# Context loaded a unit at a time, single buffers for queries, keys and output, and a new order of the first units' preparation

## The chip, the cores and the metric

The kernel is one program on one core of a Trainium2 chip. Its time is the device time of one launch in microseconds (us); lower is better. Each kernel is run several times and the median is compared.

## What is computed

```python
# x: (8, 512, 2048); ctx, the context: the same shape; mask: (8, 1, 2048), all ones
x = x + tanh(g_xattn[0]) * xattn(layernorm(x), ctx, mask, Wq, bq, Wk, bk, Wv, bv, Wo, bo)
x = x + tanh(g_ffn[0]) * ffn(layernorm(x), router_weight, router_bias, expert_bias)

def xattn(qk, v, masks, ...):      # patches of 128 columns, 8 heads of 32 rows
    q = Wq @ qk_patch + bq;  k = Wk @ qk_patch + bk;  val = Wv @ v_patch + bv
    scores = q^T k / sqrt(32), masked;  attn = softmax(scores)
    return (Wo @ gelu(attn @ val) + bo) * masks

def ffn(h, ...):                   # 4096 rows of 2048; 64 experts, the best 8 kept
    scores = softmax(h @ router_weight^T + router_bias);  w = top 8 of scores, else 0
    return h * sum(w) + w @ expert_bias
```

The weight products of the attention are done in three float32r products each (high by high, low by high, high by low), so every operand of them exists as a high part (a rounding copy) and a low part (operand minus high part).

## The kernel before

A batch is one of the 8 slices of x, held whole in SBUF as `X[b % 2]`, 128 partitions by 4 tiles by 2048 columns. It is cut into 8 units of 256 columns (two patches), 64 units in all. The order of the work on each engine is fixed by a table of due times (`SLOTS`, in slots; a unit starts every 16 slots, a batch every 128; a tick is an eighth of a slot). Each engine walks the same list of ticks and issues what is due, so the table sets only the order on an engine; semaphores set the times. Unit u's due time is 16 u plus the slot of the table; in the steady state one slot is close to one microsecond.

The path of one unit:

- GpSimd normalises the columns (`z_full`); ScalarE makes `z_hi` (`z_high`), GpSimd `z_lo` (`z_low`).
- TensorE projects queries and keys (`project`); ScalarE evicts the queries into `q32` (`q_full`), VectorE the keys into `k32` (`k_full`); each has two buffers.
- SyncE loads the context a patch at a time (`load_ctx`, 256 KB, pieces of 512 bytes) into two patch buffers `cx`; ScalarE makes `cx_hi` (`c_high`), GpSimd `cx_lo` (`c_low`), TensorE the values (`v_mm`), ScalarE evicts them (`v_full`). A load waits until the low part of the patch that was in its buffer is made.
- TensorE makes the scores (`scores`), first the mask rows from `sel`, which a DMA brings from `rows_d`; VectorE takes the maxima (`top`), ScalarE the exponentials (`expo`), VectorE transposes them in blocks (`turn_p`, `turn_d`), and SyncE moves the blocks from `T` to `PT` by 16 DMAs of 80 KB (`move`).
- TensorE weighs the values by `PT` (`weigh`), VectorE divides into `o32` (`divide`, two buffers), ScalarE takes the gelu and the high part (`gelu`, `o_high`), GpSimd the low part (`o_low`), TensorE projects out (`project_out`), VectorE and GpSimd add to x (`weigh_out`, `add_x`). Statistics and router products follow.

After a batch's last unit come its router and its mixture: VectorE adds the mixture to x and SyncE stores x by 16 DMAs of 256 KB (`store`). Then the x of the batch after the next is loaded into the same buffer in eight halves of 512 KB (`load_x`, due at slot 48.5 of the next batch and every 4 slots); VectorE takes its statistics in 16 pieces (`input_stats`, from slot 63.25, every 2 slots) and then `input_norm` (slot 101.25), on VectorE the aggregates, on GpSimd the reciprocal root. SyncE's list also holds the `sel` rows, the mask (`load_weight`) and the second batch's x (from slot 21, every 7 slots).

At the start all weights pass through `X[1]`. Four blocks in the list of ticks prepare the rest of them: VectorE at `SPLIT` (the router weights' mean taken off, their low part, the output weights scaled), ScalarE at `SPLIT_A` (`wr2` high part) and `LATE_A` (`wo_hi`, `eb2`), VectorE at `LATE_V` (`wo_lo`, low part of `eb2`). `SPLIT` stands before the first `top`, and in it VectorE waits for ScalarE's `wr2`; `LATE_A` stands before the first `expo` and waits for VectorE's scaled output weights.

## Time and profile before

| | |
|---|---|
| median of 3 runs | 1191.13 us (1187.13 to 1192.66) |
| the profiled execution | 1187.5 us, its span 1185.7 us |
| busy: TensorE matmul | 1125.4 us, 95% of the span |
| busy: ScalarE, VectorE, GpSimd | 1029.7, 946.8, 715.3 us |
| DMA engines | q1, the queue of all data, 60.6% of the 16 engines' span; 199.39 MB |
| DMAs that SyncE issues | 1018 of 80 KB from T to PT, 128 context loads of 256 KB, 64 x loads, 128 stores |
| mean granted TensorE clock | 0.988 of full speed |

Busy time is a sum over an engine's instructions; an engine at 95% over the whole span can be idle for long in one stage and saturated in all others, so the stages have to be read one by one. The time of a run stands 1.8 us over the span.

### The profile page before, as it was taken

To read this page: it belongs to the slowest core of one execution; us is meant where nothing else is said; L and a number is where in the kernel's file an instruction comes from. 1 tells how busy PE (TensorE), PEld (TensorE's weight loads), DVE (VectorE), ACT (ScalarE), POOL (GpSimd) and SP (SyncE) were. 2 spreads that over 40 slices of the span, in tenths; PEclk is the share of its full clock that TensorE was granted. 3 is DMA by queue.
4 is the path that set the end of the run, shared out by engine and by line. 5 is a ranking of instruction groups with operands and counts; after the bars stand their busy time and mean duration, and the time that the engine had idled before them with its cause. 6 is when DMAs were issued, how large, how long until landed. Compare 5 with 4: busy or idle time off the path is not lost.

```text
span 1185.7 us, 32708 instructions
## 1 busy us (share of the span) xinstructions
PE 1125.4 (95%) x11661; PEld 1044.7 (88%) x11661; DVE 946.8 (80%) x1833; ACT 1029.7 (87%) x3200; POOL 715.3 (60%) x684
## 2 busy tenths in 40 slices
PE   2699999999999999999999999998999999999976
PEld 2699999899998999898998999988999899989965
DVE  6658877998789977889778987887778997787766
ACT  3688999999999899988999999997899989998954
POOL 2366767477655667567764676746766567755621
PEclk9899999999999999999999999999999999999989
DMA  9368454786548854587456865488454885555433
GB/s 289 76 176 220 117 131 126 242 211 155 132 122 259 228 129 127 149 261 191 125 129 212 237 162 128 123 259 224 102 132 121 258 232 130 127 164 179 116 83 143
DMA packets 160162, 199.39 MB, mean 168 GB/s; under 512 B 26496, under 2 KB 102272, under 8 KB 159872
## 3 DMA queue, kind: packets, MB, share of 16 engines
q1 hardware_dynamic: 158848, 196.80, 60.6%
q8 instruction: 93, 1.52, 0.5%
q10 hardware_dynamic: 1152, 0.50, 0.2%
q14 instruction: 69, 0.57, 0.2%
HBM read 79.67 MB, written 33.65 MB: 96 GB/s over the span
## 4 chain that ended last, share of the span: by engine, by line
PE 64%; SPq 9%; ACT 9%; DVE 6%; issue 4%; POOL 4%; DMA 3%; ACTq 0%; DVEq 0%; POOLq 0%
PE ring L308 8%; SPq L519 8%; PE ring L310 7%; PE ring L309 7%; PE ring L365 4%; PE ring L323 4%; PE ring L384 4%; PE ring L348 4%; PE ring L325 4%; PE ring L324 4%; PE ring L385 4%; PE ring L386 4%; ACT T L616 3%; PE ring L403 3%; PE PR L416 2%
## 5 line engine op out<-in xcount | busy, mean ns | idle before, releaser
L616 ACT ACTIVATE T<-ring,nmx 128x128 f32<-128x128 f32 x1024 | 359.6, 406 | 30.5 <-DVE nmx L769 30.3
L308 PE MATMUL ring<-z_hi,wqk_hi 128*128 128x256 f32 x1024 | 298.9, 292 | 23.7 <-DVE z_lo L951 21.6
L309 PE MATMUL ring<-z_hi,wqk_lo 128*128 128x256 f32 x1024 | 291.7, 285 | 0.0
L310 PE MATMUL ring<-z_lo,wqk_hi 128*128 128x256 f32 x1024 | 291.7, 285 | 0.0
L616 ACT ACTIVATION_READ_ACCUMULATOR T<-ring,nmx 128x1 f32 x1024 | 251.0, 245 | 0.0
L1041 POOL TENSOR_TENSOR z_lo<-z,z_hi 128x1024 fp32r<-128x1024 f32 x62 | 147.7, 2382 | 165.2 <-ACT z_hi L584 165.2
L308 PEld LDWEIGHTS ring<-z_hi,wqk_hi 128*128 128x128 f32 x1024 | 197.6, 193 | 36.5 <-DVE wqk_lo L927 21.6
L775 DVE STREAM_TRANSPOSE T<-T 128x512 f32<-128x512 f32 x256 | 171.5, 694 | 54.2 <-ACT T L616 53.7
L1053 POOL TENSOR_TENSOR X<-X,xt 128x512 f32<-128x512 f32 x128 | 165.9, 1296 | 60.7 <-DVE xt L802 60.5
L310 PEld LDWEIGHTS ring<-z_lo,wqk_hi 128*128 128x128 f32 x1024 | 198.2, 194 | 0.0
L309 PEld LDWEIGHTS ring<-z_hi,wqk_lo 128*128 128x128 f32 x1024 | 198.0, 193 | 0.0
L1047 POOL TENSOR_TENSOR cx_lo<-cx,cx_hi 128x512 fp32r<-128x512 f32 x128 | 165.7, 1295 | 43.1 <-ACT cx_hi L600 43.1
L769 DVE TENSOR_REDUCE nmx<-ring 128x4 f32<-128x512 f32 x256 | 158.7, 683 | 17.1 <-PE ring L348 17.1
L1058 POOL TENSOR_TENSOR ot_lo<-o,ot_hi 128x512 fp32r<-128x512 f32 x63 | 81.8, 1299 | 142.8 <-ACT ot_hi L643 142.8
L323 PE MATMUL ring<-wv_hi,cx_hi 128*128 128x256 f32 x512 | 146.4, 286 | 8.1 <-POOL cx_lo L1047 8.1
L802 DVE SCALAR_TENSOR_TENSOR xt<-ring,cst,mg 128x256 f32<-128x256 f32 x256 | 111.6, 478 | 47.3 <-PE ring L386 45.8
L384 PE MATMUL ring<-ot_hi,wo_hi 128*128 128x256 f32 x504 | 143.0, 284 | 2.7 <-POOL ot_lo L1058 2.1
L324 PE MATMUL ring<-wv_lo,cx_hi 128*128 128x256 f32 x512 | 145.4, 284 | 0.0
L325 PE MATMUL ring<-wv_hi,cx_lo 128*128 128x256 f32 x512 | 145.4, 284 | 0.0
L386 PE MATMUL ring<-ot_lo,wo_hi 128*128 128x256 f32 x504 | 142.6, 283 | 0.0
L385 PE MATMUL ring<-ot_hi,wo_lo 128*128 128x256 f32 x504 | 142.3, 282 | 0.0
L1034 POOL TENSOR_SCALAR z<-X,nm,rs 128x256 f32<-128x256 f32 x252 | 138.6, 567 | 0.8
(134 smaller groups left out, 2671.5 us busy)
## 6 DMA issues: line engine op xcount, KB each, us to landing
PT<-T SPq DMA_DIRECT2D x1018, 80.0 KB, 2.1
X<-in_x SPq DMA_DIRECT2D x64, 512.0 KB, 5.6
cx<-in_ctx SPq DMA_DIRECT2D x128, 256.0 KB, 3.9
out_y<-X SPq DMA_DIRECT2D x128, 256.0 KB, 3.2
mg<-in_mask SPq DMA_DIRECT2D x64, 128.0 KB, 3.6
sel<-rows_d SPq DMA_DIRECT2D x128, 3.0 KB
X<-in_eb SPq DMA_DIRECT2D x2, 512.0 KB, 8.6
X<-in_wqT SPq DMA_DIRECT2D x1, 512.0 KB, 5.2
```

What stands on the lines that cost most here:

```text
L308: e.matmul(o, wqk_hi[:, t, cols], z_hi[:, t, :], t == 0, False)
L309: e.matmul(o, wqk_lo[:, t, cols], z_hi[:, t, :], False, False)
L310: last = e.matmul(o, wqk_hi[:, t, cols], z_lo[:, t, :], False, t == DT - 1)
L323: e.matmul(o, cx_hi[:, k, :], wv_hi[:, k, :], k == 0, False)
L324: e.matmul(o, cx_hi[:, k, :], wv_lo[:, k, :], False, False)
L325: last = e.matmul(o, cx_lo[:, k, :], wv_hi[:, k, :], False, k == DT - 1)
L384: e.matmul(o, wo_hi[:, m, cols], o_hi[:, m, :], m == 0, False)
L385: e.matmul(o, wo_lo[:, m, cols], o_hi[:, m, :], False, False)
L386: last = e.matmul(o, wo_hi[:, m, cols], o_lo[:, m, :], False, m == 1)
L616: last = e.activation(T[u % 2][:, :, n, :], bank("S", 4 * u + g)[:, k * W:(k + 1) * W].rearrange("p (b j) -> p b j", b=4), ACT.Exp, bias=n ...
L775: e.transpose(blocks, blocks).then_inc(tp_v, 1)
L1053: e.tensor_tensor(xs, xs, xt[j][:], ALU.add).then_inc(x1_g, 1)
```

## The change

Seven edits:

1. `cx` becomes two buffers of a whole unit (256 columns). One DMA of 512 KB, in pieces of 1 KB, loads a unit; 64 loads in place of 128. The load of unit u + 2 stands where the load of the second patch stood and waits for both low parts of unit u. At the start both buffers are loaded, 1 MB where 512 KB were.
2. `q32`, `k32` and `o32` have one buffer each, so `q_full`, `k_full` and `divide` wait for the reader of the unit before.
3. `onef`, `wrs`, `swb` and `ex` are placed inside `L`, and `c_logits` waits for the batch before to be done with `ex`.
4. The part of VectorE's `SPLIT` block that prepares weights moves behind the first `top` (`SET_V`, tick 9), without the low part of `wr2`, which moves to `LATE_V`. So that block waits for ScalarE no more.
5. `LATE_V` moves from tick 50 to 140, behind the second unit's `top`; ScalarE's `SPLIT_A` from tick -39 to 60 and `LATE_A` from 24 to 90, both behind the first `expo`. The counts that others wait for follow (`v_w` 5 and 6 are exchanged).
6. `c_high` of patch 3 is written at a tick of its own (`CTX_A`, 39); it stood at 42, and nothing of ScalarE's list lies between.
7. The x halves are loaded from slot 50.75, every 5 slots, and their statistics taken from slot 65.75, every 2.25 slots; `input_norm` stays at 101.25.

```diff
@@ -52,9 +52,9 @@
-    sx=44.75, sx_gap=1.25, x2=45.25, rl=48.5, rl_gap=4,
-    x_1=21, x_gap=7, bn1=63.25, bn1_gap=2, norm1=101.25,
+    sx=44.75, sx_gap=1.25, x2=45.25, rl=50.75, rl_gap=5,
+    x_1=21, x_gap=7, bn1=65.75, bn1_gap=2.25, norm1=101.25,
@@ -95,7 +95,7 @@
-        NC, NV, NR, NO = 2, 4, 7, 2
+        NC, NV, NR, NO = 2, 4, 7, 1
@@ -110,11 +110,11 @@
-        cx = [sb(f"cx{i}", [128, DT, W]) for i in range(NC)]
+        cx = [sb(f"cx{i}", [128, DT, U]) for i in range(NC)]
-        q32 = [sb(f"q32_{i}", [128, 2, U]) for i in range(2)]
-        k32 = [sb(f"k32_{i}", [128, 2, U]) for i in range(2)]
+        q32 = sb("q32", [128, 2, U])
+        k32 = sb("k32", [128, 2, U])
@@ -144,20 +144,18 @@
-        swb = sb("swb", [128, NX])
+        onef, wrs, swb = L[:, 0:128], L[:, 128:128 + NX], L[:, 256:256 + NX]
-        ex = sb("ex", [128, DT, NX])
+        ex = L[:, 256:512].rearrange("p (t x) -> p t x", t=DT)
-        onef = sb("onef", [128, 128])
-        wrs = sb("wrs", [128, NX])
@@ -208,8 +206,8 @@
-        SPLIT, SPLIT_A = -48, -39
-        LATE_V, LATE_A, NEXT_A, NEXT_V = 50, 24, -40, -49
+        SPLIT, SPLIT_A, SET_V = -48, 60, 9
+        LATE_V, LATE_A, NEXT_A, NEXT_V, CTX_A = 140, 90, -40, -49, 39
@@ -345,7 +343,7 @@
-                            last = e.matmul(o, q32[u % 2][head, m, cols], k32[u % 2][head, m, cols], False, w == 1 and m == 1)
+                            last = e.matmul(o, q32[head, m, cols], k32[head, m, cols], False, w == 1 and m == 1)
@@ -408,7 +406,7 @@
-                    e.wait_ge(v_w, 5)
+                    e.wait_ge(v_w, 6)
@@ -457,7 +455,7 @@
-                    e.matmul(PR[:, 0:NX], onef[:], wrs[:], True, True).then_inc(pe_set, 1)
+                    e.matmul(PR[:, 0:NX], onef, wrs, True, True).then_inc(pe_set, 1)
@@ -487,11 +485,11 @@
-            def load_ctx(p):
-                b, w = divmod(p, S // W)
-                if p >= NC:
-                    e.wait_ge(cxlo_g, p - NC + 1)
-                e.dma_start(cx[p % NC][:], cv[b][:, :, w * W:(w + 1) * W]).then_inc(cx_in[p % NC], 16)
+            def load_ctx(u):
+                b, c = divmod(u, NU)
+                if u >= NC:
+                    e.wait_ge(cxlo_g, 2 * (u - NC) + 2)
+                e.dma_start(cx[u % NC][:], cv[b][:, :, c * U:(c + 1) * U]).then_inc(cx_in[u % NC], 16)
@@ -539,8 +537,8 @@
-            for p in range(NC):
-                load_ctx(p)
+            for u in range(NC):
+                load_ctx(u)
@@ -555,10 +553,9 @@
-                for w in range(2):
-                    for u in due(t, (8 + C["v_gap"]) * w + C["c_lo"]):
-                        if 2 * u + w + NC < TP:
-                            load_ctx(2 * u + w + NC)
+                for u in due(t, 8 + C["v_gap"] + C["c_lo"]):
+                    if u + NC < TU:
+                        load_ctx(u + NC)
@@ -584,20 +581,21 @@
-                if u >= 2:
-                    e.wait_ge(s_pe, u - 1)
+                if u:
+                    e.wait_ge(s_pe, u)
-                e.activation(q32[u % 2][:, 0, :], bank("q", u)[:, 0:U], ACT.Identity, bias=cst[:, BQ:BQ + 1])
-                e.activation(q32[u % 2][:, 1, :], bank("q", u)[:, U:2 * U], ACT.Identity,
+                e.activation(q32[:, 0, :], bank("q", u)[:, 0:U], ACT.Identity, bias=cst[:, BQ:BQ + 1])
+                e.activation(q32[:, 1, :], bank("q", u)[:, U:2 * U], ACT.Identity,
-                e.wait_ge(cx_in[p % NC], 16 * (p // NC + 1))
-                e.activation(cx_hi[:], cx[p % NC][:], ACT.Copy).then_inc(cxhi_a, 1)
+                u, w = divmod(p, 2)
+                e.wait_ge(cx_in[u % NC], 16 * (u // NC + 1))
+                e.activation(cx_hi[:], cx[u % NC][:, :, w * W:(w + 1) * W], ACT.Copy).then_inc(cxhi_a, 1)
@@ -652,6 +650,7 @@
+                    e.wait_ge(w2_v, b)
@@ -712,12 +711,14 @@
-                    e.wait_ge(v_w, 6)
+                    e.wait_ge(v_w, 5)
+                if t == CTX_A:
+                    c_high(3)
@@ -726,7 +727,8 @@
-                        c_high(2 * u + w)
+                        if 2 * u + w != 3:
+                            c_high(2 * u + w)
@@ -755,10 +757,10 @@
-                if u >= 2:
-                    e.wait_ge(s_pe, u - 1)
+                if u:
+                    e.wait_ge(s_pe, u)
-                e.tensor_tensor(k32[u % 2][:], bank("k", u)[:].rearrange("p (m i) -> p m i", m=2),
+                e.tensor_tensor(k32[:], bank("k", u)[:].rearrange("p (m i) -> p m i", m=2),
@@ -859,7 +861,7 @@
-                e.tensor_tensor(low(b), low(b), ex[:], ALU.mult).then_inc(wm_v, 1)
+                e.tensor_tensor(low(b), low(b), ex, ALU.mult).then_inc(wm_v, 1)
@@ -914,7 +916,7 @@
-            e.memset(onef[:], 1.0).then_inc(v_set, 1)
+            e.memset(onef, 1.0).then_inc(v_set, 1)
@@ -957,17 +959,15 @@
-            e.tensor_reduce(wrs[:], wrst.rearrange("p k n -> p n k"), AX.X, ALU.add).then_inc(v_m, 1)
+            e.tensor_reduce(wrs, wrst.rearrange("p k n -> p n k"), AX.X, ALU.add).then_inc(v_m, 1)
-                if t == SPLIT:
+                if t == SET_V:
-                    e.tensor_scalar(swb[:], PR[:, 0:NX], -1.0 / S, None, ALU.mult).then_inc(v_m, 1)
+                    e.tensor_scalar(swb, PR[:, 0:NX], -1.0 / S, None, ALU.mult).then_inc(v_m, 1)
-                    e.tensor_tensor(wrst, wrst, swb[:].unsqueeze(1).to_broadcast([128, SB, NX]), ALU.add).then_inc(v_m, 1)
+                    e.tensor_tensor(wrst, wrst, swb.unsqueeze(1).to_broadcast([128, SB, NX]), ALU.add).then_inc(v_m, 1)
-                    e.wait_ge(a_w, 4)
-                    e.tensor_tensor(wr2[:, :, NX:2 * NX], wrst, f32(wr2[:, :, 0:NX]), ALU.subtract).then_inc(v_w, 1)
@@ -975,6 +975,8 @@
+                    e.wait_ge(a_w, 4)
+                    e.tensor_tensor(wr2[:, :, NX:2 * NX], wrst, f32(wr2[:, :, 0:NX]), ALU.subtract).then_inc(v_w, 1)
@@ -1044,7 +1046,8 @@
-                e.tensor_tensor(cx_lo[:], cx[p % NC][:], f32(cx_hi[:]), ALU.subtract).then_inc(cxlo_g, 1)
+                u, w = divmod(p, 2)
+                e.tensor_tensor(cx_lo[:], cx[u % NC][:, :, w * W:(w + 1) * W], f32(cx_hi[:]), ALU.subtract).then_inc(cxlo_g, 1)
```

## Rows read from the trace of the kernel before

**Rows 1.** Windows of the start: length, busy (count) by engine, granted clock, DMA share, GB/s

```profile
16.00:20.00 4.00, 0.00 (x0) 0.00 (x0) 2.09 (x8) 1.38 (x2) 1.50 (x3) 1.00 1.08 349
20.00:40.00 20.00, 16.85 (x143) 16.43 (x144) 15.21 (x18) 8.62 (x15) 8.79 (x9) 1.00 0.71 164
40.00:60.00 20.00, 11.34 (x95) 10.70 (x94) 13.18 (x18) 15.74 (x68) 8.16 (x10) 0.78 0.29 76
```

**Rows 2.** Timeline of TensorE, the first units: start, length, what, idle before

```profile
33.28 1.06 PE L348 MATMUL ring<-k,q 32*128 32x128 f32 x32
...
50.07 0.55 PE L323 MATMUL ring<-wv_hi,cx_hi 128*128 128x256 f32 x1 [6.59 <-POOL cx_lo L1047]
...
56.97 0.36 PE L308 MATMUL ring<-z_hi,wqk_hi 128*128 128x256 f32 x1 [2.06 <-POOL z_lo L1041]
...
62.92 1.08 PE L365 MATMUL ring<-PT,v 128*32 128x128 f32 x32
```

**Rows 3.** Timeline of VectorE, the blocks around the first maxima

```profile
33.84 0.22 DVE L964 TENSOR_SCALAR swb<-PR 128x64 f32<-128x64 f32 x1
...
37.58 1.75 DVE L972 TENSOR_SCALAR X<-X,cst 128x1024 f32<-128x1024 f32 x1
39.26 2.47 DVE L769 TENSOR_REDUCE nmx<-ring 128x4 f32<-128x512 f32 x4
...
42.89 2.35 DVE L981 SCALAR_TENSOR_TENSOR eb<-X,cst,eb 64x2048 fp32r<-64x2048 f32 x1
```

**Rows 4.** Timeline of ScalarE, before and behind the first exponentials

```profile
39.37 1.06 ACT L716 ACTIVATE wo_hi<-X 128x1024 fp32r<-128x1024 f32 x1 [2.17 <-DVE X L972]
40.33 2.00 ACT L718 ACTIVATE eb<-X,cst 128x2048 fp32r<-128x2048 f32 x1
...
47.80 0.71 ACT L600 ACTIVATE cx_hi<-cx 128x512 fp32r<-128x512 f32 x1
...
53.29 1.05 ACT L584 ACTIVATE z_hi<-z 128x1024 fp32r<-128x1024 f32 x1
```

**Rows 5.** Timeline of SyncE's queue: the first mask rows, the first move

```profile
24.59 1.35 SPq L509 DMA_DIRECT2D sel<-rows_d  x4
...
50.43 10.82 SPq L519 DMA_DIRECT2D PT<-T  x16
```

**Rows 6.** TensorE's waits over the span: total, times, longest

```profile
PE ring L365 <- DMA PT<-T: 7.5, 7, 3.8
```

**Rows 7.** Timeline of TensorE, `weigh` of four successive units, 42 to 45

```profile
790.73 1.08 PE L365 MATMUL ring<-PT,v 128*32 128x128 f32 x32
...
806.64 1.08 PE L365 MATMUL ring<-PT,v 128*32 128x128 f32 x32
...
826.86 1.93 PE L365 MATMUL ring<-PT,v 128*32 128x128 f32 x32 [3.83 <-DMA PT<-T]
...
845.37 1.08 PE L365 MATMUL ring<-PT,v 128*32 128x128 f32 x32
```

**Rows 8.** SyncE's queue before the latest move of a batch

```profile
804.99 1.49 SPq L526 DMA_DIRECT2D X<-in_x  x3
...
809.50 0.43 SPq L494 DMA_DIRECT2D cx<-in_ctx  x1
810.04 11.01 SPq L519 DMA_DIRECT2D PT<-T  x16
```

**Rows 9.** Landing of the 16 DMAs of that move, from the line's own view

```profile
DMA to landing us min/median/max: 3.7/5.1/7.2
```

**Rows 10.** Window of that move, columns as in group 1

```profile
816.00:827.00 11.00, 6.96 (x61) 6.58 (x63) 7.92 (x14) 9.72 (x38) 7.38 (x9) 0.95 0.99 230
```

**Rows 11.** Timelines behind `input_norm`: GpSimd, SyncE's queue, TensorE

```profile
422.66 1.30 POOL L1047 TENSOR_TENSOR cx_lo<-cx,cx_hi 128x512 fp32r<-128x512 f32 x1
...
424.48 11.09 SPq L519 DMA_DIRECT2D PT<-T  x16
...
437.22 1.08 PE L365 MATMUL ring<-PT,v 128*32 128x128 f32 x32 [0.33 <-DMA PT<-T]
```

## The prediction, made before the changed kernel ran

> **What bounds the kernel now.** I read the windows of the span first. Behind the start TensorE is busy almost without a break (95% of the whole span, the table above); what a change can win is in its breaks. The end isn't touched. At the start the windows show 3.1 us idle of the 20 us to 40 us, and 8.7 us of the next 20, with the granted clock at 0.78 there [rows 1]. TensorE's timeline says what ended the idle time: the values of patch 3 waited 6.6 us for `cx_lo`, the queries of unit 2 another 2.1 us for `z_lo` [rows 2]. Followed back over the other engines: `cx_lo` waited for `c_high`, which stands behind the first `expo` on ScalarE; `expo` stood behind `wo_hi` and `eb2` and behind the maxima; the maxima start at 39.26 us though their scores ended at 34.34 us, because VectorE was in the `SPLIT` block from 33.84 us on [rows 2 to 4].
>
> In the middle, the list of TensorE's waits has one of weight: `weigh` on the moves to `PT`, 7.5 us in 7 waits [rows 6]. The worst costs more than its wait: two undisturbed `weigh` are 15.9 us apart, the next two distances are 20.2 and 18.5 us, so 6.9 us are lost, of them 3.8 us idle and 3.1 us after or around it at the lower clock [rows 7]. 7.5 + 3.1 = 10.6 us of the middle can be had back at most.
>
> **The start, step by step.** Time zero is the old timeline.
>
> *The mask rows come later.* The extra 512 KB of context stands in SyncE's queue before the mask rows (`sel`) of the first scores, and DMA was saturated then, at 349 GB/s in one window; in a later saturated one it moved 230 [rows 1, 10]. 0.52 MB by these is 1.5 to 2.3 us. The old rows were issued from 24.59 to 25.94 us; the first scores started about 33.1 us, right behind other work, so the landing isn't seen; it can have had some slack, at most half a microsecond by my estimate, from the 7 us that it then still had to land behind 1 MB of `eb` [rows 2, 5]. So the scores come 1.0 to 2.3 us later; I take 1.6. The nearest row is the 349 one, at the same stage, less a little slack: hence a value in the lower half. The Trainium skill (DMA: Bandwidth & Descriptors, section Specifications) gives 435 GB/s as the fabric's ceiling; by that the delay would be 1.2 us and the start would win 0.4 us more. The window shows that this queue didn't reach it.
>
> *The first maxima.* The scores then end at 35.9 us; the maxima follow at once, at 36.0 us in place of 39.26. `expo` needs the first of four, 0.7 us on, and ScalarE has nothing else left before it: 36.7 us, where it stood at 42.3 us, behind `eb2` [rows 3, 4]. Its length is unchanged, 5.5 us (42.33 to 47.80), so `c_high` of patch 3 starts at 42.2 us, 5.6 us earlier [rows 4]. It needs context that is loaded at the start. TensorE then still waits for `cx_lo`, but about 1 us.
>
> *ScalarE behind it.* `wr2`, `wo_hi` and `eb2` now stand between `c_high` and `z_high` of unit 2: about 1.0 + 1.0 + 1.9 us (starts of the rows apart, the first like the second) [rows 4]. With `c_high` (0.55), the evictions of a patch, the queries and the next patch (0.3 + 0.7 + 0.3), `z_high` starts at 42.2 + 3.9 + 1.85 = 47.95, where it stood at 53.29: 5.3 us earlier. The three blocks cost nothing more because ScalarE had idled there for patch 3's product.
>
> *VectorE behind it.* Maxima to 38.5 us; the moved block, without the wait and the `wr2` subtraction, 0.25 + 1.15 + 0.2 + 1.7 = 3.3 us [rows 3], to 41.8; four transposes and the denominators 3.6 us, to 45.4; then the move, at 45.4 us in place of 50.43: 5.0 us earlier [rows 5]. The old one waited in the queue for `c_low` of patch 3 and the load behind it; that is ready by about 44.5 us now. The move's last DMA plus its landing came just at the first `weigh`, at 62.92 us [rows 2], so this is the smaller of the two shifts and sets the win: **5.0 us**. With the delay of the mask rows at 0 it is 6.6, at 2.3 us it is 4.3. If unit 2's projections run at the higher clock after a shorter pause, they then wait for the move, so that adds nothing.
>
> *`LATE_V`.* Three subtractions, 1.2 + 1.2 + 2.35 = 4.8 us [rows 3], now stand between the second `top` and its transposes. They lie under the second `expo` (5.5 us); with the transposes behind them they end about 3 us later than that, near 58 us. The second move wouldn't start sooner: it stands behind the load that waits for `c_low` of patch 5, and that follows the product of patch 4, just before the first `weigh` (57.9 us), by 0.7 and 1.3 us: 59.9 us. Without that cover it would cost the 3 us. `project_out` and `load_x` of the second batch, which wait for the subtractions, come later still.
>
> **The middle.** *The latest move.* Each batch's move due at slot 72.5 stood behind four x halves and two context loads since the move before; now behind three halves and one double load. In the batch with the long wait, three halves took 1.49 us of issue, a context load 0.43 [rows 8]: the move starts 0.5 + 0.4 us earlier, less 0.2 for the place of the move before. The bytes in front of it shrink by 512 KB, 2.3 us at the window's 230 GB/s [rows 10]. The landings there, median 5.1 and up to 7.2 us [rows 9], should shrink so. 0.7 + 2.3 = 3.0 us of the 3.8 go, and with so short a pause the clock shouldn't fall: 3.0 + 3.1 = 6.1 us. The same place has two more waits of 2.0 us together (in the 7.5 us of [rows 6]) that vanish. Sum **-8.1 us**; between 0, if bytes don't decide, and -10.
>
> *The later statistics.* `input_norm` keeps its place, but two of the 16 pieces, 0.6 us each, now stand between `top` and the aggregates, and one of them before the second `xt`. GpSimd's root waits for the aggregates, the context's low part stands behind the root, SyncE's load waits for that and the move stands behind the load: low part to 423.96, move from 424.48, landed just when `weigh` started, after 0.33 us of idle [rows 11]. So there is no slack, and each of the 7 batches with an `input_norm` pays what reaches GpSimd: 0 to 1.2 us; I take 0.6, the one piece before `xt`, in each: **+4.0 us**.
>
> *The x half just before a move.* At slot 56.5 the move now stands directly behind context and x (1 MB) and starts 0.5 us later. The bytes are as before and the 16 issues take 11 us, in which the queue drains; I take +0.5 us over all batches, up to +4.
>
> *Costed at nothing.* Half the context issues are gone, 64 x 0.43 = 27 us of SyncE's issue time, but SyncE isn't what TensorE waits for outside these places. Single `q32`, `k32`, `o32`: the evictions stand 12 to 16 slots behind the old readers, hidden by the scores and by `o_low`; without that cover each unit would pay one eviction, 0.7 us. The tiles in `L` are read a batch before or behind its writers.
>
> **Sum.** -5.0 - 8.1 + 4.0 + 0.5 = -8.6 us, so 1178.9 us against the profiled 1187.5. That execution lies 3.6 us under the median of the runs. Waits on the moves differ from run to run and would explain that; with most of them gone I expect the new median close to the sum: **1179.5 us**.
>
> **The rivals.**
> (a) *Only the start wins.* The waits on the moves stay, because the queue, not the last 512 KB, decides: 1191.1 - 5.0 = 1186 us. For it: DMA share is 0.99 in that window either way [rows 10]. Against: landings of 5.1 us for 80 KB say that bytes stand in front of them [rows 9]. With the statistics' 4 us on top it would be 1190.
> (b) *Both win fully.* The mask rows were never late, the pieces of statistics fit: 1187.5 - 6.6 - 10 = 1171 us. Against: [rows 11].
> (c) *Slower.* The move at slot 56.5 lands behind the 1 MB in front of it. Without its term the sum is 1178.4; it decides once each of the 6 batches that load x pays over 2.1 us (1191 us), and 3.1 us make it slower by 0.5%. At 3.5 us each, half a wait like that of [rows 7], the time is 1199 us, with all of it 1220. [...] Against it: its last DMA is issued 10.5 us after the x half.
> (d) *The start wins nothing*, since the second unit's chain (ScalarE's 3.9 us of moved work) takes the place of the first's, and the middle goes as forecast: 1187.5 - 3.6 = 1184 us.
>
> **How the numbers follow.** Forecast 0.58, (a) 0.15, (b) 0.10, (c) 0.08, (d) 0.09. A change of 0.5% (6 us) is about what a measurement of this kernel can tell from none; the line lies at 1185.2 us. The forecast and (b) are faster, two thirds of (d) and two fifths of (a): 0.80. Same: the rest of (a) and (d), 0.13. Slower 0.07. The range reaches from (b), 1171, to just over (a), 1187.
>
> **What would show it.** The first maxima near 36 us and the first `weigh` near 58 us; if they come near 34.5, the mask rows had slack. The waits of `weigh` on `PT` under 4 us in all, none followed by a lower clock. The aggregates of `input_norm` 0.6 to 1.2 us nearer to the move behind them, and a short wait in each batch there. Wrong would be: scores that wait for `sel` over 3 us, waits on `PT` one unit earlier in each batch than before, or unit 2's projections waiting for `z_lo` as long as now.

## The result

| | before | changed |
|---|---|---|
| median of 10 runs each | 1186.86 us (1182.51 to 1193.57) | 1182.15 us (1180.15 to 1185.24) |
| ratio | 1 | 0.9947, 95% interval 0.9927 to 0.9968 |
| profiled execution, span | 1187.5, 1185.7 us | 1182.08, 1180.3 us |
| TensorE busy | 1125.4 us | 1122.0 us |

The change makes the kernel about half a per cent faster: 4.7 us between the medians, 5.4 between the profiled executions, and the runs lie closer together (5 us apart, 11 before). The median of before is 4 us under the one that the prediction started from; it had three runs then. In one run of all those reported here the chip was in a slow state (1362.33 us, at 0.753 of the full clock); that run is left out of every number.

The windows of the start in the changed kernel, in the columns of [rows 1]:

```profile
20.00:40.00 20.00, 17.41 (x152) 17.06 (x153) 14.72 (x20) 10.99 (x39) 9.55 (x11) 1.00 0.73 189
40.00:60.00 20.00, 14.60 (x147) 13.79 (x146) 17.02 (x21) 16.40 (x56) 12.30 (x8) 0.83 0.47 126
```

TensorE's idle time in these 40 us fell from 11.8 to 8.0 us. Its timeline, against [rows 2]:

```profile
33.77 0.40 PE L337 MATMUL ring<-sel,ones 32*128 32x512 bf16 x4 [1.24 <-DMA sel<-rows_d]
33.99 1.07 PE L346 MATMUL ring<-k,q 32*128 32x128 f32 x32
...
43.64 0.36 PE L321 MATMUL ring<-wv_hi,cx_hi 128*128 128x256 f32 x1 [1.20 <-POOL cx_lo L1050]
...
50.72 0.55 PE L306 MATMUL ring<-z_hi,wqk_hi 128*128 128x256 f32 x1 [4.20 <-POOL z_lo L1043]
...
57.75 1.08 PE L363 MATMUL ring<-PT,v 128*32 128x128 f32 x32
```

The wait in the first line is new: the scores wait for the mask rows. These were issued later already, at 25.91 us where it had been 24.59, because the DMA of the expert biases before them held SyncE longer. In SyncE's queue, before and then changed:

```profile
20.31 3.52 SPq L549 DMA_DIRECT2D X<-in_eb  x1
20.39 4.76 SPq L547 DMA_DIRECT2D X<-in_eb  x1
```

The values of patch 3 come 6.4 us earlier, unit 2's queries 6.3 us, the first `weigh` 5.2 us. VectorE, against [rows 3]:

```profile
35.12 2.48 DVE L771 TENSOR_REDUCE nmx<-ring 128x4 f32<-128x512 f32 x4 [1.97 <-PE ring L346]
...
49.00 2.65 DVE L979 TENSOR_TENSOR wr<-X,wr 128x1024 fp32r<-128x1024 f32 x1
51.57 2.31 DVE L981 TENSOR_TENSOR wo_lo<-X,wo_hi 128x1024 fp32r<-128x1024 f32 x1
53.92 2.53 DVE L983 SCALAR_TENSOR_TENSOR eb<-X,cst,eb 64x2048 fp32r<-64x2048 f32 x1
```

The maxima start 4.1 us earlier, and the first two of the three subtractions behind them take about twice as long as before (1.2 us each then). Beside the three stand, in GpSimd's timeline:

```profile
48.22 2.35 POOL L1043 TENSOR_TENSOR z_lo<-z,z_hi 128x1024 fp32r<-128x1024 f32 x1 [4.73 <-ACT z_hi L581]
50.52 2.27 POOL L1050 TENSOR_TENSOR cx_lo<-cx,cx_hi 128x512 fp32r<-128x512 f32 x1
52.78 5.18 POOL L1036 TENSOR_SCALAR z<-X,nm,rs 128x256 f32<-128x256 f32 x4
```

In the middle TensorE's waits on the moves ([rows 6]) have become longer in sum and shorter each; from its list of waits:

```profile
PE ring L363 <- DMA PT<-T: 9.7, 14, 1.7
```

Of the units of [rows 7], number 44, which had waited 3.8 us, waits half a microsecond, and no slow stretch follows it. TensorE's timeline:

```profile
806.49 1.08 PE L363 MATMUL ring<-PT,v 128*32 128x128 f32 x32 [0.28 <-DMA PT<-T]
...
823.01 1.08 PE L363 MATMUL ring<-PT,v 128*32 128x128 f32 x32 [0.52 <-DMA PT<-T]
...
838.93 1.08 PE L363 MATMUL ring<-PT,v 128*32 128x128 f32 x32
```

Behind the norm, in the batch of [rows 11], the timelines of four engines one after the other. VectorE:

```profile
414.08 0.69 DVE L908 BATCH_NORM_STATS2 bnst<-X 128x6 f32<-128x512 f32 x1
414.68 0.86 DVE L804 SCALAR_TENSOR_TENSOR xt<-ring,cst,mg 128x256 f32<-128x256 f32 x2
415.46 0.68 DVE L908 BATCH_NORM_STATS2 bnst<-X 128x6 f32<-128x512 f32 x1
```

GpSimd:

```profile
415.62 1.29 POOL L1056 TENSOR_TENSOR X<-X,xt 128x512 f32<-128x512 f32 x1 [1.09 <-DVE xt L804]
...
420.81 1.29 POOL L1050 TENSOR_TENSOR cx_lo<-cx,cx_hi 128x512 fp32r<-128x512 f32 x1
```

SyncE's queue:

```profile
422.13 0.40 SPq L492 DMA_DIRECT2D cx<-in_ctx  x1
422.64 11.57 SPq L517 DMA_DIRECT2D PT<-T  x16
```

TensorE:

```profile
435.86 1.08 PE L363 MATMUL ring<-PT,v 128*32 128x128 f32 x32 [1.14 <-DMA PT<-T]
```

A piece of the statistics (`bnst`) now stands right in front of the second `xt`; GpSimd waits 1.09 us for `xt` where it had waited 0.49, the low part ends at 422.10 us, the load is issued behind it and the move behind the load; `weigh` waits 1.14 us, where it had waited 0.33. What is late is the start of the move and not its landing. The last of its 16 DMAs, by the view of its line, takes no longer than before:

```profile
DMA to landing us min/median/max: 2.1/2.1/2.1
```

That holds for the last DMA of the move in all seven units behind a norm, in both kernels; the moves start 11.7 to 12.1 us before TensorE is ready for them, where it had been 12.2 to 12.9.

To see where the 5.1 us by which the last `weigh` comes earlier went, I took the start of `weigh` of each of the 64 units in both traces and the distance from one to the next. Most distances are 15.92 us in both. These differ:

| place | units | changed less before, us |
|---|---|---|
| up to the first `weigh` | 0 | -5.2 |
| second batch's x is loaded | 1, 2, 3 | +0.3, +1.3, -1.0 |
| behind a norm (slot 121.25) | 6, 14, 22, 30, 38, 46, 54 | +0.75, +0.64, +1.07, +0.50, +0.15, +0.41, +0.74: +4.3 |
| before the latest move | 27, 35, 43 | +0.28, +0.37, +0.37: +1.0 |
| latest move and the one behind | 12, 20, 28, 36, 44, 45 | -0.4, +1.1, -1.0, +0.5, -3.7, -2.6: -6.0 |

### The profile page after: what moved, and what is told of

It is laid out like the page before. It is cut to its first block, busy times and chain, and to the rows that moved or that the text cites. A ratio compares the mean times of both kernels' runs of the same rounds, so it can differ in the third digit from the quotient of the medians.

```text
span 1180.3 us, 32647 instructions
## 1 busy us (share of the span) xinstructions
PE 1122.0 (95%) x11661; PEld 1041.2 (88%) x11661; DVE 947.0 (80%) x1833; ACT 1028.4 (87%) x3200; POOL 718.7 (61%) x684
## 2 busy tenths in 40 slices
DMA packets 126369, 199.37 MB, mean 169 GB/s; under 512 B 25472, under 2 KB 68480, under 8 KB 126080
## 4 chain that ended last, share of the span: by engine, by line
PE 49%; SPq 15%; DVE 11%; ACT 9%; issue 6%; POOL 5%; DMA 4%; ACTq 0%; DVEq 0%; POOLq 0%
SPq L517 12%; PE ring L306 6%; PE ring L308 5%; PE ring L307 5%; ACT T L614 4%; PE ring L363 4%; PE ring L346 3%; PE ring L382 3%; PE ring L383 3%; PE ring L384 3%; DMA PT<-T 3%; PE ring L321 3%; PE ring L322 3%; PE ring L323 3%; PE ring L401 2%
## 5 line engine op out<-in xcount | busy, mean ns | idle before, releaser
L1036 POOL TENSOR_SCALAR z<-X,nm,rs 128x256 f32<-128x256 f32 x252 | 141.2, 578 | 0.8
```

## The experiments

All ratios are against the kernel before, run beside the experiment on the same chip, with 95% intervals. Comparisons between experiments go by medians; the kernel before itself stood between 1189.1 and 1189.9 us there. Beside the changed kernel it stood at 1186.86. So the changed kernel's 1182.15 us is 1 to 3 us too low to be set beside the medians of the experiments; where this matters, the difference by the ratios is given too, as a share of 1189 us.

### The three parts alone

**Only the context** (edits 1 to 3), in the changed kernel with the others undone. The instructions that stand at these ticks move back with them.

```diff
-    sx=44.75, sx_gap=1.25, x2=45.25, rl=50.75, rl_gap=5,
+    sx=44.75, sx_gap=1.25, x2=45.25, rl=48.5, rl_gap=4,
-    x_1=21, x_gap=7, bn1=65.75, bn1_gap=2.25, norm1=101.25,
+    x_1=21, x_gap=7, bn1=63.25, bn1_gap=2, norm1=101.25,
-        SPLIT, SPLIT_A, SET_V = -48, 60, 9
-        LATE_V, LATE_A, NEXT_A, NEXT_V, CTX_A = 140, 90, -40, -49, 39
+        SPLIT, SPLIT_A = -48, -39
+        LATE_V, LATE_A, NEXT_A, NEXT_V = 50, 24, -40, -49
...
```

> Only edits 1 to 3 on the kernel before: context a unit at a time, single buffers, tiles inside L; the old order at the start and the old times of the x halves. My theory: the context edit buys TensorE nothing, since SyncE's saved issues lie where nothing waits for them, and it costs the mask rows about 1.2 us at the start (the first scores wait for sel), so the first weigh comes at 63 to 64 us and the time is 0 to 2 us above that of the kernel before. The moves that come right behind 512 KB may add up to 1 us. The rival: larger pieces and fewer DMAs relieve the queue, the waits of weigh on PT fall under 4 us in all and the time is 3 to 5 us below.

Measured: 1187.32 us, ratio 0.9986 (0.9961 to 1.0010). First `weigh` at 63.40 us, 9.6 us of waits on `PT`. By itself this part is worth nothing that can be told from zero. The first `weigh` lies within my theory's 63 to 64 us, 0.5 us later than before, but not by its way: in TensorE's timeline the scores start at 33.34 us without a wait for `sel`. Neither theory's time holds clearly, as the interval reaches from -0.4% to +0.1%. The longest wait, 5.2 us, is at unit 43, one unit ahead of the one in [rows 7].

**Only the order at the start** (edits 4 to 6), in the kernel before.

```diff
-        SPLIT, SPLIT_A = -48, -39
-        LATE_V, LATE_A, NEXT_A, NEXT_V = 50, 24, -40, -49
+        SPLIT, SPLIT_A, SET_V = -48, 60, 9
+        LATE_V, LATE_A, NEXT_A, NEXT_V, CTX_A = 140, 90, -40, -49, 39
...
+                if t == CTX_A:
+                    c_high(3)
...
```

> Only edits 4 to 6: the new order of the first units' preparation, with context by patches and everything else as before. My theory: the start is all of the gain that is certain, and without the extra 512 KB ahead of the mask rows it is larger: the first scores follow their predecessor without a wait, the first weigh comes at 56.3 to 57 us (62.92 before, 57.75 in the changed kernel), and the time is 6.2 us below that of the kernel before, give or take what the waits on PT do in the middle. The rival: the 5.2 us of the changed kernel need the whole unit of context in SBUF early; then patch 3 comes late and the first weigh stays at 60 us or more.

Measured: 1183.68 us, ratio 0.9954 (0.9931 to 0.9977). In its timeline of TensorE the scores follow without a wait, and the first `weigh` comes at 57.08 us:

```profile
33.57 0.40 PE L339 MATMUL ring<-sel,ones 32*128 32x512 bf16 x4
...
50.52 0.55 PE L308 MATMUL ring<-z_hi,wqk_hi 128*128 128x256 f32 x1 [4.19 <-POOL z_lo L1044]
...
57.08 1.08 PE L365 MATMUL ring<-PT,v 128*32 128x128 f32 x32
```

The start gives 5.8 us of the 6.2 expected. By the ratios (0.9954, and 0.9947 for the changed kernel) it is nearly the whole of the changed kernel's gain. The rival is out: the start doesn't need the context early.

This kernel has the middle of the kernel before, unchanged, and its trace shows how much of the 3.8 us wait of [rows 7] was that one execution. The same `weigh` of unit 44 here:

```profile
823.68 1.08 PE L365 MATMUL ring<-PT,v 128*32 128x128 f32 x32 [0.36 <-DMA PT<-T]
```

The units 44 and 45 are 6.4 us shorter than in the profiled execution of before, though no edit touches them, and the waits on `PT` are 12.3 us in all.

**Only the x halves and their statistics** (edit 7), in the kernel before.

```diff
-    sx=44.75, sx_gap=1.25, x2=45.25, rl=48.5, rl_gap=4,
+    sx=44.75, sx_gap=1.25, x2=45.25, rl=50.75, rl_gap=5,
...
-    x_1=21, x_gap=7, bn1=63.25, bn1_gap=2, norm1=101.25,
+    x_1=21, x_gap=7, bn1=65.75, bn1_gap=2.25, norm1=101.25,
```

> Only edit 7: x halves and their statistics later and farther apart. My theory: it removes the long wait at the latest move of a batch, which differs from run to run (6 us in the profiled execution of before), and pays 0.6 us in each of 7 batches behind the norm of the next x: weigh of the units 6, 14, 22, 30, 38, 46 and 54 each come 0.4 to 1.1 us later against their predecessors. Net between -3 and +3 us, with a smaller spread of the runs than before. The rival: the 0.4 to 1.1 us come from the context's 512 KB right ahead of the move, not from the statistics; then these units are as before here and the time is 5 us or more below.

Measured: 1188.05 us, ratio 0.9976 (0.9952 to 0.9999). The waits behind the norms are all there, with 256 KB right ahead of the move as before, and not 512: the units 6, 14, 22, 29 with 30, 38, 46 and 54 lose 1.4, 0.3, 1.4, 1.5, 0.4, 1.3 and 0.2 us, 6.6 together. One of them:

```profile
439.89 1.08 PE L365 MATMUL ring<-PT,v 128*32 128x128 f32 x32 [1.76 <-DMA PT<-T]
```

So edit 7 causes them, and the rival is out. The long wait of unit 44 is 0.9 us here. The net is 1 us by the medians, within the -3 to +3 expected.

### What holds the move behind a norm

**The load behind the move.**

```diff
-                for u in due(t, 8 + C["v_gap"] + C["c_lo"]):
+                for u in due(t, C["mv"] - 16):
                     if u + NC < TU:
                         load_ctx(u + NC)
```

> The changed kernel with one line moved: a unit's context load stands behind the move in SyncE's queue, not before it, so the move no longer waits for the context's low part and has no 512 KB right ahead of it. My theory: the waits of weigh on PT in the units behind a norm (4.3 us of the changed kernel against before) come through that load; they go altogether, with the 1.0 us of the units before the latest move. 4 to 7 us below the changed kernel, waits on PT 3 us or less in all. The rival: these moves are late because their transposes are late or because the queue is full; then it makes under 1 us.

Measured: 1178.89 us, ratio 0.9908 (0.9878 to 0.9939); first `weigh` at 55.29 us. Its waits:

```profile
PE ring L363 <- DMA PT<-T: 6.3, 3, 3.1
```

All three are in the units 19, 27 and 43; behind the norms nothing is lost but 0.4 us in unit 54. SyncE's queue behind the norm of the same batch shows why:

```profile
415.77 11.45 SPq L517 DMA_DIRECT2D PT<-T  x16
427.26 0.59 SPq L492 DMA_DIRECT2D cx<-in_ctx  x1
```

And TensorE's timeline:

```profile
430.32 1.08 PE L363 MATMUL ring<-PT,v 128*32 128x128 f32 x32
```

The last of the 16 is issued by 427.2 us, 3.1 us ahead of `weigh`, since the move no longer stands behind a load that waits for GpSimd. In the seven units behind a norm the moves now start 14.3 us or more before TensorE is ready, and their last DMAs again land after 2.1 us (3.0 in unit 54): so it was the wait in the queue that held them, and not the bytes of the load. The median is 3.3 us under the changed kernel's, 4.6 us by the ratios; I had expected 4 to 7 and waits of 3 us or less, and hadn't foreseen that other waits would grow. I hadn't counted the start either: the first `weigh` comes 2.5 us earlier, of which 1.4 are there at the first maxima already (33.74 us), ahead of the first move and so of the edit's effect. The waits that grew are at the move due at slot 56.5, which follows the stores and two x halves directly. Before the one of unit 43 the queue reads:

```profile
771.32 11.61 SPq L529 DMA_DIRECT2D out_y<-X  x16
782.97 0.48 SPq L498 DMA_DIRECT2D mg<-in_mask  x1
783.54 1.08 SPq L524 DMA_DIRECT2D X<-in_x  x2
784.73 11.62 SPq L517 DMA_DIRECT2D PT<-T  x16
```

The last DMA of this move took 6.5 us to land, where it was 2.7 in the changed kernel. What made it slower isn't separated. With the 3.15 us wait went another 1.5 us in the next distance, at a granted clock of 0.90.

**All statistics earlier.**

```diff
-    x_1=21, x_gap=7, bn1=65.75, bn1_gap=2.25, norm1=101.25,
+    x_1=21, x_gap=7, bn1=63, bn1_gap=2.25, norm1=101.25,
```

> The changed kernel with one number changed: the statistics of x start at slot 63 in place of 65.75, so that the last of the 16 pieces stands ahead of the maxima before the norm and none between the maxima and the aggregates. The x halves stay later. My theory: VectorE's two pieces there are what made the second xt, GpSimd's root, the context's low part and with it the move 0.6 us later; the waits of the units 6, 14, 22, 30, 38, 46, 54 (4.3 us against before) shrink to 0 to 0.3 each, the time by 2 to 4 us against the changed kernel. The rival: the 512 KB right ahead of that move cause them; then those waits stay and the time is the same.

Measured: 1210.52 us, ratio 1.0167 (1.0140 to 1.0195): a miss. VectorE's timeline shows a piece that stands in front of the transposes and whose x half has not landed:

```profile
262.97 0.69 DVE L908 BATCH_NORM_STATS2 bnst<-X 128x6 f32<-128x512 f32 x1 [4.34 <-DMA X<-in_x]
263.58 2.47 DVE L777 STREAM_TRANSPOSE T<-T 128x512 f32<-128x512 f32 x4
```

In sum, from VectorE's waits:

```profile
DVE bnst L908 <- DMA X<-in_x: 32.7, 11, 5.3
```

Such a piece holds the transposes of the unit back, with them the move, and each of the six batches loses about 5 us (units 13, 21, 29, 37, 45, 53). The half is issued behind the move due at slot 72.5; the piece, number 10 of 16 counted from 0, stood at slot 88.25, behind the transposes, and now at 85.5, ahead of them. It answers another question than I had asked: halves that come later need statistics that come later, so the two numbers of edit 7 belong together. The first batch, where no piece waits for its half, does answer what I had asked. There the two last pieces stand ahead of the maxima, none stands behind them, and GpSimd waits for the second `xt` as long as in the changed kernel (1.08 us there):

```profile
135.27 1.30 POOL L1056 TENSOR_TENSOR X<-X,xt 128x512 f32<-128x512 f32 x1 [1.10 <-DVE xt L804]
```

Unit 6 still loses 0.9 us against before. The next run asks the same of all batches.

**The last two pieces alone.**

```diff
-                    for b in due(t, C["bn1"] + C["bn1_gap"] * i, 128, NB - 1):
+                    at = C["bn1"] + C["bn1_gap"] * i if i < 14 else 96.5 + 0.25 * (i - 14)
+                    for b in due(t, at, 128, NB - 1):
```

> The changed kernel with only the last two of the 16 pieces of statistics moved, from slots 97.25 and 99.5 to right ahead of the maxima at 97; their x half landed long before. This is the clean form of the test that starting all statistics earlier was meant to be (that one met x halves that had not landed). My theory: the second xt comes 0.6 us and the aggregates 1.2 us earlier behind the maxima; GpSimd, the context's low part, the load and the move follow; of the 4.3 us that the units 6, 14, 22, 30, 38, 46, 54 lost against before, 2 to 4 come back, and the time falls by as much. Against it: the maxima themselves come up to 1.2 us later, which delays the exponentials and the transposes ahead of that same move. The rival: 512 KB right ahead; then nothing changes.

Measured: 1186.23 us, ratio 0.9974 (0.9951 to 0.9996), 4 us above the changed kernel (3.2 by the ratios). VectorE's timeline in the same batch as above:

```profile
410.98 1.86 DVE L908 BATCH_NORM_STATS2 bnst<-X 128x6 f32<-128x512 f32 x3
412.76 2.46 DVE L771 TENSOR_REDUCE nmx<-ring 128x4 f32<-128x512 f32 x4
415.15 0.86 DVE L804 SCALAR_TENSOR_TENSOR xt<-ring,cst,mg 128x256 f32<-128x256 f32 x2
```

GpSimd's:

```profile
416.09 1.29 POOL L1057 TENSOR_TENSOR X<-X,xt 128x512 f32<-128x512 f32 x1 [1.69 <-DVE xt L804]
...
421.25 1.29 POOL L1051 TENSOR_TENSOR cx_lo<-cx,cx_hi 128x512 fp32r<-128x512 f32 x1
```

The pieces ahead of the maxima make the maxima 1.06 us later and the second `xt` 0.47, though one piece fewer stands between the two; GpSimd follows `xt`, and the low part ends 0.44 us later. The units behind the norms lose another 4.1 us. So the remedy fell, and what I had feared beside it decided. The chain is the one of the theory: it is the second `xt`, with any piece ahead of it, that GpSimd waits for.

**Is edit 7 needed once the load stands behind the move?** The changed kernel with both edits:

```diff
-    sx=44.75, sx_gap=1.25, x2=45.25, rl=50.75, rl_gap=5,
+    sx=44.75, sx_gap=1.25, x2=45.25, rl=48.5, rl_gap=4,
...
-    x_1=21, x_gap=7, bn1=65.75, bn1_gap=2.25, norm1=101.25,
+    x_1=21, x_gap=7, bn1=63.25, bn1_gap=2, norm1=101.25,
...
-                for u in due(t, 8 + C["v_gap"] + C["c_lo"]):
+                for u in due(t, C["mv"] - 16):
```

> The changed kernel with the context load behind the move, and the x halves and statistics at their old, closer times (edit 7 undone). It asks what edit 7 is worth once the context is out of the way. My theory: with four halves ahead of the latest move the waits of the units 12, 20, 28, 36, 44, 52 come back, 0.4 to 1.5 us each and at times one of 4 us with a lower clock behind it; 2 to 5 us above the kernel with the load behind the move. The rival: without the 512 KB of context ahead of it that move has room for a fourth half, and the earlier statistics are better; same time or 1 us below.

Measured: 1177.76 us, ratio 0.9907 (0.9878 to 0.9935), with 4.1 us of waits on `PT`. The rival was right: with the context out of the way, edit 7 is worth nothing (1178.89 with it).

### The mask rows

```diff
+            load_rows(0)
             e.dma_start(ebst[0:NX, :], eb).then_inc(sm_eb, 16)
             e.dma_start(ebst[NX:128, :], eb).then_inc(sm_eb, 16)
...
-                    load_rows(n)
+                    if n:
+                        load_rows(n)
```

> The changed kernel with the first mask rows' DMA ahead of the 1 MB of expert biases in SyncE's queue. My theory: the first scores waited 1.24 us for these rows because of what is ahead in the queue; now they don't wait, the first weigh comes at about 56.6 us (57.75) and the time is 1 us less. The rival: the first weigh is held by the move's own chain (low part of patch 3, load, 16 issues), which doesn't shift; then nothing changes. The queue waits some 2 us for the rows to be written out, so the biases land later; they are read at 44 us, which leaves over 8 us.

Measured: 1181.73 us, ratio 0.9938 (0.9912 to 0.9965); the wait for `sel` is gone and the first `weigh` comes at 56.18 us, 1.6 earlier. In the profiled executions the last `weigh` is 1.6 us earlier too, though in between single units differ by up to 1.6 us both ways. The medians differ by 0.4 us (1.1 by the ratios), which the spread of the runs doesn't tell from 1.6.

**All three together** (load behind the move, statistics from slot 63, mask rows first).

```diff
-    x_1=21, x_gap=7, bn1=65.75, bn1_gap=2.25, norm1=101.25,
+    x_1=21, x_gap=7, bn1=63, bn1_gap=2.25, norm1=101.25,
...
+            load_rows(0)
...
-                for u in due(t, 8 + C["v_gap"] + C["c_lo"]):
+                for u in due(t, C["mv"] - 16):
...
```

> The changed kernel with the context load behind the move, the statistics from slot 63 and the first mask rows ahead of the biases. My theory: the first gave 3.3 us by its medians against the changed kernel, the rows give 1.2 more, the earlier statistics nothing, since the move no longer stands behind GpSimd's work: 1177 to 1178 us where the kernel with the first alone has 1178.9, and a first weigh at 54 us. The rival: the earlier statistics meet x halves that haven't landed; VectorE then waits and the gain is gone.

Measured: 1209.60 us, ratio 1.0173 (1.0145 to 1.0201). It fell to the rival, as the kernel with the earlier statistics alone did.

**The version that the runs point to**: the load behind the move, edit 7 undone, the mask rows first.

> The version that the runs so far point to: the changed kernel with the context load behind the move, the old times of the x halves and their statistics, and the first mask rows ahead of the biases. My theory: 1177.8 us of the kernel without the last edit less about 1 us: 1176 to 1177.5. First weigh at 54 to 55 us. The rival: the first moves are then held by their own 16 issues; no difference to the kernel without the last edit (1176.8 to 1183.2 us).

Measured: 1176.52 us (1173.80 to 1181.78), ratio 0.9892 (0.9865 to 0.9920), the fastest of all and faster than both kernels; 2.4 us of waits on `PT` are left. The last edit's 1.2 us between the medians are as expected, but within the spread of six runs. The profiled executions don't show them: the first `weigh` comes at 56.16 us, not at 54 to 55 as expected, and at 56.50 without the edit. So what the mask rows are worth once the load stands behind the move stays open.

### One DMA or two

The context of a unit by two DMAs of 256 KB at the same place, first by patches, in pieces of 512 bytes (a unit's row of 256 floats is cut in two).

```diff
-                e.dma_start(cx[u % NC][:], cv[b][:, :, c * U:(c + 1) * U]).then_inc(cx_in[u % NC], 16)
+                for w in range(2):
+                    e.dma_start(cx[u % NC][:, :, w * W:(w + 1) * W],
+                                cv[b][:, :, c * U + w * W:c * U + (w + 1) * W]).then_inc(cx_in[u % NC], 16)
...
-                e.wait_ge(cx_in[u % NC], 16 * (u // NC + 1))
+                e.wait_ge(cx_in[u % NC], 32 * (u // NC + 1))
```

> The changed kernel with each unit of context loaded by two DMAs of 256 KB in pieces of 512 bytes, one right behind the other at the same place in the queue, in place of one DMA of 512 KB in pieces of 1 KB. It measures the size of the DMA by itself. My theory: it costs 0.45 us of SyncE's issue time in each unit ahead of the move, where the move has no slack behind a norm (7 units) and in the units 20 to 44 that wait: 1 to 4 us slower. The rival: the size is worth nothing, within 1 us of the changed kernel; or it is worth what the changed kernel won in the middle, then over 5 us slower.

Measured: 1195.22 us (1189.64 to 1201.38, 11 runs), ratio 1.0045 (1.0022 to 1.0069): 13.1 us above the changed kernel, 11.7 by the ratios. That is far over the 1 to 4 us of my theory and on the rival's side (over 5). Then by pairs of tiles, in the pieces of 1 KB that the one DMA has:

```diff
-                e.dma_start(cx[u % NC][:], cv[b][:, :, c * U:(c + 1) * U]).then_inc(cx_in[u % NC], 16)
+                for h in range(2):
+                    e.dma_start(cx[u % NC][:, 2 * h:2 * h + 2, :],
+                                cv[b][:, 2 * h:2 * h + 2, c * U:(c + 1) * U]).then_inc(cx_in[u % NC], 16)
...
-                e.wait_ge(cx_in[u % NC], 16 * (u // NC + 1))
+                e.wait_ge(cx_in[u % NC], 32 * (u // NC + 1))
```

> The changed kernel with each unit of context in two DMAs of 256 KB as before, but cut by tiles of rows, so that the pieces stay 1 KB. The kernel with two DMAs and 512-byte pieces lay 13 us above the changed kernel by its median. If the number of DMAs does it (0.55 us of SyncE's issue time ahead of every move, my theory), this one is slower by as much: 8 to 14 us above the changed kernel, waits on PT 15 us or more. If the length of the pieces does it, this one is within 2 us of the changed kernel.

Measured: 1188.30 us (1185.37 to 1200.62), ratio 0.9999 (0.9971 to 1.0028): 6 us above the changed kernel, between the two expectations. TensorE's waits on `PT` with short pieces:

```profile
PE ring L363 <- DMA PT<-T: 18.5, 18, 2.2
```

And with long ones:

```profile
PE ring L363 <- DMA PT<-T: 24.4, 19, 3.9
```

Both count: the second DMA some 6 us, the short pieces some 7 more by the medians, 5.5 by the ratios. The profiled executions stand the other way round (1192.45 and 1198.7 us), so one profile of these kernels doesn't order them; the runs do.

## Why the prediction was right, and where it wasn't

**The start: -5.0 forecast, -5.2 measured**, and its times came within 1.4 us: maxima at 35.1 us (36.0), `cx_hi` of patch 3 at 41.4 (42.2), `z_hi` of unit 2 at 46.9 (47.95), the move at 44.0 (45.4). The mask rows did come late, and the first scores started 0.7 us later than before; the term was 1.6. They waited 1.24 us, but everything ahead of them ran 0.5 us earlier in this execution. One step was another than forecast. VectorE's moved block took 2.3 us and not 3.3, and the transposes ended at 43.2 us; what held the move last was the load in front of it, which waited for a low part that ended at 43.5. With the load behind and edit 7 undone the first move starts right behind its transposes, at 43.29 us, and the first `weigh` comes at 56.50. That only the move's chain sets the win fits with unit 2's queries, which came 6.3 us earlier and bought nothing more. The edits of the order alone bring the win by themselves, so this cause is shown.

**`LATE_V`: 4.8 us forecast, 7.4 measured** (49.00 to 56.45 us), since GpSimd's `z_lo`, `cx_lo` and `z_full` ran at the same time and the two engines held each other up (last section). The cover held, but only just: the transposes ended at 59.85 us, where near 58 was forecast, and the low part that the load waited for at 59.92. The second move started at 60.43 us, behind the load, near the 59.9 of the forecast. The units 1 and 2 lost 1.6 us, which the next one gave back for 1.0. Unit 2's part of it, 1.3 us, is missing in three of the four other kernels with the same start (statistics earlier, last two pieces, two DMAs with short pieces), so it looks like chance; it wasn't separated.

**The latest move: -8.1 forecast, -6.0 measured.** The long wait and its slow stretch went, 6.3 us for 6.1, but that agreement is luck. The kernel with the order of the start alone, whose middle nobody changed, lost the same 6.4 us there: the forecast took one execution's wait for a cost of every execution. What edit 7 does at this place is smaller. The waits of the units 12, 20, 28, 36, 44 and 52 sum to 6.1 us before and 8.5 us with the start's order alone; with edit 7 they sum to 1.9 us by itself, and to 3.4, 2.3 and 4.2 us in the changed kernel and in two more that load context and x as it does (mask rows first, last two pieces). So some 2 to 7 us of waits go, by one execution each. And units 20 and 36, which should have lost their waits, lost 1.1 and 0.5 us more. The step that failed is that the waits shrink with the bytes in front, and vanish: in unit 20 the move started 0.4 us earlier against its `weigh`, with half a megabyte less in front of it since the last move, and its last DMA took 5.3 us to land where it had taken 4.3. The kernel with the load behind the move shows those waits gone in all six units. There the move of unit 20 starts 16.7 us before TensorE is ready, where it was 14.0, and the landing falls to 3.5 us; which of the two does it, the earlier start or the 512 KB that no longer stand right ahead, isn't separated for these units.

**The statistics: +4.0 forecast, +4.3 measured**, by the way it was worked out: one piece ahead of the second `xt`, 0.6 us, in GpSimd's timeline as a wait of 1.09 us. The size is partly luck: the single units lost 0.15 to 1.07 us, and with the mask rows first, where the middle is the same, the seven units lost 6.0 us. The edit with x alone shows the loss without the context, the edit of the load shows that it acts through SyncE's queue, and the landings of 2.1 us show that the load's bytes have no part in it.

**The x half just before a move: +0.5 forecast, +1.0 measured**, within the bounds. Rival (c), which lived by this place, decides from 2.1 us in each batch; the units 27, 35 and 43 lost 0.3 to 0.4. They are the sign that the prediction had named as wrong, waits one unit earlier than before, in three batches of six and small.

**Costed at nothing**: half the context issues. That was wrong as it was put. The move has so little slack in the batches' busy stretch that one DMA more ahead of it costs about 6 us and short pieces 5 to 7, if both loads stand there. Where the patches' loads stand apart, as before, they cost far less: the context edit alone is worth 0 to 0.4%. The single buffers and the tiles in `L` don't show as a wait in TensorE's or VectorE's list.

**The sum**: -5.2 + 0.6 - 6.0 + 4.3 + 1.0 = -5.3 us; forecast -8.6, and the difference is the latest move (2.1), the units 1 to 3 (0.6), the rest of half a microsecond. The predicted 1179.5 us stand 2.7 over-optimistic against 1182.15, and the old median of 1191.13 us was a high draw: its ten runs gave 1186.86. That the waits on the moves differ from run to run is shown by the traces of kernels with the same middle; that there are fewer in the changed kernel, as its narrower spread suggests, isn't: one sign of the prediction was waits on `PT` under 4 us in all, and they were 9.7, where before had 7.5.

**What was luck.** The runs put the middle at nearly nothing, where -3.6 us were forecast (-8.1 + 4.0 + 0.5): the start's order alone has the ratio 0.9954, with the other edits on top 0.9947, some 0.8 us apart. The size of the change is thus that of rival (a), only the start wins, -5.0 us, and its waits on the moves did stay. That 1182.15 us lies nearer to the forecast than to its 1186 comes from the old median, 4 us too high. The other two parts alone measured 0.9986 and 0.9976; all three multiplied would give 0.9916, so together they may cost 0.3%, which their intervals don't tell from nothing.

## What to carry to other kernels

Ask of every wait in a DMA queue what stands behind it: here the load's wait for GpSimd held a move that had no reason to wait, and moving one line was worth another 3 to 5 us, nearly as much as the whole change. Don't forecast from a wait that one profile shows: look for it in a second execution with that stage untouched. When a buffer becomes deep enough that its load has a unit of slack, put the load behind the urgent DMAs. Place work that is moved on an in-order engine by what it waits for (an x half) as much as by what waits behind it.

## What the runs showed of the hardware

- Subtractions of 128x1024 took 1.23 and 1.21 us in the kernel before and 2.65 and 2.31 us in the changed one, where GpSimd's `z_lo` and `cx_lo` ran beside them. They overlap as if each stood until the other had ended: `z_lo` ended at 50.57 us and VectorE's subtraction at 51.65, `cx_lo` at 52.79 and the next subtraction at 53.88, each about 1.1 us behind the other. `cx_lo` took 2.27 us, where it takes 1.29 later on, and GpSimd's four normalisations 5.18 us, most of it beside VectorE's last two subtractions, where they take 2.18 us at 418.67. The Trainium skill (GPSIMD Engine Reference, section 1. Specifications) has GpSimd's SBUF interfaces shared with VectorE, with contention for instructions of two SBUF inputs; the trace agrees for these, which read two tensors. The kernel with the start's order alone shows the same times (2.65, 2.30 and 5.18 us).
- The median landing of the 80 KB moves was 2.3 to 2.5 us in the kernels that have the context's 512 KB right ahead of the move, and 2.1 to 2.2 us in those that load by patches or have the load behind. Some 34,000 packets fewer (126369 for 160162) didn't lower it.
- A DMA can land before one issued ahead of it in the same queue: the load issued at 422.13 us landed after 5.1 us, and the move's first DMA, issued at 422.64 us, after 4.0. The first DMA of that move was slower than the last (2.1 us).
- A wait of 3.8 us lost 6.9 us (rows 7). In the changed kernel waits up to 1.7 us were followed by distances of 15.92 us, at the full clock. Between the two it varied: after 3.15 us (load behind the move) the next distance lost 1.5 us more at a granted clock of 0.90, after 2.71 us (start's order alone, unit 3) none.
